# ScalarE's prelude reordered: the square root's table first, the small tanh behind the queries' copies, one table for logarithm and exponential

## The chip, the cores and the metric

The kernel is one program on one core of a Trainium2 chip. The metric is device time in microseconds, from launch to the end of the program, lower is better. The kernel before took 744.48 us as the median of three runs (744.48, 745.78 and 743.02). One execution, the one of 743.02 us, was also recorded by the hardware profiler.

The core has five engines that each work through their own queue of instructions in order: TensorE (PE, matrix products and transposes into PSUM), VectorE (DVE), ScalarE (ACT), GpSimd (POOL) and SyncE (SP, which here issues all transfers). They meet only at semaphores: one instruction counts a semaphore up when it ends (`then_inc`), another engine's queue stands still until the count is reached (`wait_ge`).

## The reference, cut to what matters

Inputs: `x` and `ctx` are 32 sequences of 128 tokens with 128 features in float32. Four blocks are added to `x` one after the other, each scaled by the tanh of one scalar gate (`g_xattn[0]`, `g_ffn[0]`, `g_xattn[1]`, `g_ffn[1]`):

1. an mLSTM attention of LayerNorm(x) over ctx, with eight heads of width 16, gates capped by 15 tanh(p/15), a cumulative sum of log-sigmoids, and a norm over each head;
2. a quantized two-layer network with a gelu (hidden width 512);
3. a dynamic-time-warping alignment of ctx to LayerNorm(x): distances, a recursion over rows, a walk back;
4. a network of eight gated experts (hidden width 512, gelu).

What this case is about is the beginning of block 1:

```python
pre = gate_in @ ifgate_w.T + ifgate_b          # gate_in: [LayerNorm(x), ctx, ctx]
pre = GATE_SOFT_CAP * jnp.tanh(pre / GATE_SOFT_CAP)
log_fg = jax.nn.log_sigmoid(f_pre)             # here as -ln(1 + exp(-f))
x = x + jnp.tanh(g_xattn[0]) * _L0_xattn_ref(_layernorm(x), ctx_1024, ctx_1024, ...)
```

## The kernel before

The kernel runs its stages one after the other over all 32 sequences. Each engine's queue is written out by hand, in one function per engine (`@block.sync`, `@block.gpsimd`, `@block.scalar`, `@block.vector`, `@block.tensor`); there is no planner. Groups `g` are of four sequences, so there are eight. A tile of a group is 128 partitions by 512 columns.

The prelude (the first 62 us) makes the inputs of the attention loop. SP issues the loads: `x` and `ctx` in four chunks each (L289, L290), nine small tensors after the first chunks (L293). VectorE takes the statistics of the first 16 sequences (L841, then `ln_stats`, L741 to L747, which ends with `bn_done`), copies the turned small tensors (L846 to L848), touches `tgr` (L849, `tg_in_ready`), waits for the square root in `ln_scales` (L751), takes the reciprocal (L759) and applies the norm to 16 sequences (`ln_apply`, recorded as L735, `ln_done` after every four). The same follows for the second half of the sequences.

TensorE turns four groups of ctx (`turn_ctx`, L1364), forms the first sums of the gates from them (`ctx_sums(0)`, L1380), turns two more groups of ctx, four groups of the normed x (`turn_x`, L1372), the last two of ctx, and forms the other sums (`query_sums`, L1388). `turn_ctx(g)` waits from g = 2 on for `k_kept`, the copy two groups back, as both use the same PSUM bank.

ScalarE's queue in the prelude is what the change touches. In order: the tanh of the four scalar gates (L447, behind a wait for `tg_in_ready`), then `keep_ctx` of groups 0 and 1 (L450, copies of the turned ctx from PSUM), the square root of the first half (L443, behind `bn_done`), `keep_ctx` 2 to 5, `keep_queries` 0 to 3 (L455, two masked copies each), `keep_ctx` 6 and 7, the second square root, `keep_sums(0)` (L460), `keep_queries` 4 to 7, `keep_sums(1)`, and then the gates: tanh (L479), exponential (L481) and logarithm (L482) of the gate values, 16 squares (L485), four roundings (L495), one masked copy (L497), a named table load (L498), an exponential (L500), and two scalings (L503, L504).

ScalarE evaluates functions from a table of which one set is active at a time. A function that is not in the active set needs an instruction ACT_TABLE_LOAD before it. `act.preload_act_table_set(name)` puts one there by name; where the program names none and one is needed, it is put in when the program is compiled. Copies, squares and scalings follow every load of this trace without a load of their own.

Behind the gates: VectorE and TensorE make a cumulative sum (L1417), the running maxima (L893), and two matrices for the attention loop. TensorE runs 16 matmuls on constants in `keep_warm` (L1342) and then waits for `mblk_ready`, `part_ready` and others before the first `exponents(0)` (L1445). `mblk` is made by VectorE in four instructions at L917, recorded as L735 with output Bm.

Of the kernel before, what the change touches and what calls it, by code (L numbers as in the profile page):

```python
# [12 lines left out]
ACT = mybir.ActivationFunctionType  # L13
# [42 lines left out]
def program(nc, x, ctx_, g_x, g_f, if_w, if_b, on_w, a_w1, a_b1, a_w2, a_b2, gate_w, m_w1, m_b1, m_w2, m_b2, out):  # L56
    with ExitStack() as stack:
        def sb(name, shape, dt=F32):
            return stack.enter_context(nc.sbuf_tensor(name, shape, dt))
# [98 lines left out]
        tgr = sb("tgr", [P, 4])  # L158
        tg = sb("tg", [P, 4])
# [74 lines left out]
        def bank(n, a=0, b=512):  # L234
            return PS[:, n, a:b]
# [191 lines left out]
        def _(act):  # L427
            steps = [0]

            def link(ins):  # L430
                steps[0] += 1
                ins.then_inc(S["act_step"], 1)
                act.wait_ge(S["act_step"], steps[0])
# [9 lines left out]
                    act.activation(lnt[:, 5, 16 * h:16 * h + 16], lnt[:, 4, 16 * h:16 * h + 16], ACT.Sqrt, bias=cst[:, 0:1]).then_inc(S["ln_sqrt"], 1)  # L443

            act.sem_inc(S["h_gelu"], 4)
            act.wait_ge(S["tg_in_ready"], 1)
            act.activation(tg[:], tgr[:], ACT.Tanh).then_inc(S["tg_ready"], 1)  # L447
            def keep_ctx(g):
                act.wait_ge(S["c_turned"], g + 1)
                act.activation(kT[:, 512 * g:512 * g + 512], bank(2 + g % 2), ACT.Copy).then_inc(S["k_kept"], 1)  # L450

            def keep_queries(g):
                act.wait_ge(S["q_turned"], g + 1)
                for r in range(2):
                    ins = act.activation(qTm[:, r, 512 * g:512 * g + 512], bank(g % 2), ACT.Copy, scale=pm[:, r:r + 1])  # L455
                ins.then_inc(S["q_kept"], 1)

            def keep_sums(n):
                act.wait_ge(S["gates_summed"], n + 1)
                act.activation(sums[:, n], bank(4 + n), ACT.Copy).then_inc(S["gates_kept"], 1)  # L460
# [12 lines left out]
            keep_sums(0)  # L473
            for g in range(4, G4):
                keep_queries(g)
            keep_sums(1)

            act.wait_ge(S["gates_biased"], 1)
            act.activation(pre, pre, ACT.Tanh, scale=1.0 / GATE_CAP).then_inc(S["gates_capped"], 1)  # L479
            act.wait_ge(S["gates_capped"], 1)  # L480
            link(act.activation(nlf, pre[:, :, NH:2 * NH], ACT.Exp, scale=-GATE_CAP))  # L481
            act.activation(nlf, nlf, ACT.Ln, bias=cst[:, 3:4]).then_inc(S["nlf_ready"], 1)  # L482
            act.wait_ge(S["gates_turned"], 2)
            for b in range(B // 2):
# [10 lines left out]
                    act.activation(fl(av_cut, w), fl(av_res if r else av, w), ACT.Copy).then_inc(S["cut_done"], 1)  # L495
            act.wait_ge(S["left_over"], 3)
            act.activation(fl(av_part, 0), fl(av_res, 0), ACT.Identity, scale=pm[:, 4:5]).then_inc(S["part_ready"], 1)  # L497
            act.preload_act_table_set("natural_log_exp_and_others")  # L498
            act.wait_ge(S["m_tok_ready"], 1)
            act.activation(expnm[:], expnm[:], ACT.Exp).then_inc(S["expnm_ready"], 1)  # L500

# [1240 lines left out]
```

## Time and profile before

| what | value |
|---|---|
| median of three runs | 744.48 us |
| the profiled execution | 743.02 us |
| its span, first to last instruction | 741.1 us |
| PE busy | 569.4 us (77%) |
| DVE busy | 569.1 us (77%) |
| ACT busy | 408.5 us (55%) |
| POOL busy | 128.3 us (17%) |
| shares of the chain that ended last | PE 63%, DVE 25%, ACT 6%, issue 3% |
| mean granted clock of TensorE, 0 to 1 | 0.88 |

The span is the time between the first and the last instruction; the 1.9 us around it are launch and end. Busy shares are means over stages with different limits. In the rows further down a line of the timeline reads: start in us from the span's start, duration of the group, engine, line, operation, output, input, count, and in brackets the engine's idle time before it with what ended it. A count above one means that neighbouring instructions of a line are merged.

### The profile page before, as it was taken

To read this page: it belongs to the slowest core of one execution; us is meant where nothing else is said; L and a number is where in the kernel's file an instruction comes from. 1 tells how busy PE (TensorE), PEld (TensorE's weight loads), DVE (VectorE), ACT (ScalarE), POOL (GpSimd) and SP (SyncE) were. 2 spreads that over 40 slices of the span, in tenths; PEclk is the share of its full clock that TensorE was granted. 3 is DMA by queue.
4 is the path that set the end of the run, shared out by engine and by line. 5 is a ranking of instruction groups with operands and counts; after the bars stand their busy time and mean duration, and the time that the engine had idled before them with its cause. 6 is when DMAs were issued, how large, how long until landed. Compare 5 with 4: busy or idle time off the path is not lost.

```text
span 741.1 us, 17115 instructions
## 1 busy us (share of the span) xinstructions
PE 569.4 (77%) x6351; PEld 402.0 (54%) x6419; DVE 569.1 (77%) x1737; ACT 408.5 (55%) x766; POOL 128.3 (17%) x163
## 2 busy tenths in 40 slices
PE   2758998826544720083679999999999999999997
PEld 2433444312244620073576777777777777777776
DVE  6867788998969559997974566586877888887775
ACT  2667876678862532265445565665545454545452
POOL 3000343413000000000036777700000000000000
PEclk9959999957858975578758999999999999999999
DMA  8100000000010000041000000000000000010000
GB/s 227 42 0 1 3 3 2 2 0 0 1 56 2 2 2 0 0 119 54 0 1 1 2 1 2 2 1 2 16 1 3 14 0 15 0 42 0 15 1 16
DMA packets 19676, 12.13 MB, mean 16 GB/s; under 512 B 1149, under 2 KB 18457, under 8 KB 19609
## 3 DMA queue, kind: packets, MB, share of 16 engines
q1 hardware_dynamic: 19608, 11.25, 5.5%
q8 instruction: 40, 0.66, 0.4%
q14 instruction: 28, 0.22, 0.1%
HBM read 9.15 MB, written 2.10 MB: 15 GB/s over the span
## 4 chain that ended last, share of the span: by engine, by line
PE 63%; DVE 25%; ACT 6%; issue 3%; SPq 1%; DMA 1%; another core or an unknown queue 0%; DVEq 0%
PE PS L1649 9%; PE PS L1664 8%; PE PS L1666 8%; PE PS L1665 8%; PE PS L1650 7%; PE PS L1648 6%; DVE A L1175 3%; DVE Bm L1146 3%; PE PS L1459 3%; PE PS L1469 2%; DVE Bm L735 2%; PE PS L1577 1%; PE PS L1478 1%; DVE A L1140 1%; ACT A L455 1%
## 5 line engine op out<-in xcount | busy, mean ns | idle before, releaser
L698 ACT ACTIVATE A<-PS,small_t 128x512 f32<-128x512 f32 x256 | 168.1, 688 | 119.0 <-PE PS L1650 117.5
L1666 PE MATMUL PS<-kT_w,A 128*128 128x128 bf16 x1024 | 174.8, 219 | 0.0
L1665 PE MATMUL PS<-kT_w,A 128*128 128x128 bf16 x1024 | 174.8, 219 | 0.0
L1664 PE MATMUL PS<-kT_w,A 128*128 128x128 bf16 x1024 | 174.7, 219 | 0.0
L1277 DVE TENSOR_TENSOR A<-A 128x512 bf16<-128x512 f32 x192 | 123.6, 690 | 7.8 <-ACT A L698 6.6
L1664 PEld LDWEIGHTS PS<-kT_w,A 128*128 128x128 bf16 x1024 | 100.2, 98 | 7.4
L1665 PEld LDWEIGHTS PS<-kT_w,A 128*128 128x128 bf16 x1024 | 100.2, 98 | 7.4
L1666 PEld LDWEIGHTS PS<-kT_w,A 128*128 128x128 bf16 x1024 | 100.2, 98 | 0.0
L1649 PE MATMUL PS<-A,xn_w 128*128 128x512 bf16 (+1 forms) x256 | 97.5, 381 | 3.5 <-issue 0.2
L1650 PE MATMUL PS<-A,xn_w 128*128 128x512 bf16 (+1 forms) x256 | 97.5, 381 | 0.0
L1285 DVE SCALAR_TENSOR_TENSOR xs<-PS,A,xs 128x128 f32 (+1 forms) x192 | 54.1, 343 | 49.2 <-PE PS L1666 49.1
L1648 PE MATMUL PS<-A,xn_w 128*128 128x512 bf16 (+1 forms) x193 | 73.5, 381 | 0.0
L413 POOL TENSOR_TENSOR A<-A 128x512 bf16<-128x512 f32 x64 | 64.5, 1040 | 22.4 <-ACT A L698 22.4
L1650 PEld LDWEIGHTS PS<-A,xn_w 128*128 128x128 bf16 x256 | 25.1, 98 | 30.7 <-issue 0.8
L1585 PE MATMUL PS<-identf,Bm 64*64 64x64 f32 x2 | 0.6, 298 | 51.6 <-DVE Bm L1146 51.6
L1648 PEld LDWEIGHTS PS<-A,xn_w 128*128 128x128 bf16 x256 | 26.7, 104 | 21.1 <-issue 0.6
L1649 PEld LDWEIGHTS PS<-A,xn_w 128*128 128x128 bf16 x256 | 25.1, 98 | 21.1 <-issue 0.6
L409 POOL TENSOR_TENSOR A<-A 128x512 bf16<-128x512 f32 x8 | 9.4, 1183 | 153.3 <-ACT A L691 153.3
L1585 PEld LDWEIGHTS PS<-identf,Bm 64*64 64x64 f32 x2 | 0.2, 125 | 51.9 <-issue 49.1
L1459 PE MATMUL PS<-A,kT_w 32*128 32x256 f32 x256 | 25.4, 435 | 3.7 <-DVE A L928 3.7
L702 ACT ACTIVATE Bm<-PS 128x512 f32 x16 | 9.6, 597 | 33.3 <-PE PS L1666 33.3
L928 DVE TENSOR_TENSOR A<-Bm,PS 128x512 f32<-128x512 f32 x32 | 20.6, 684 | 7.7 <-ACT Bm L510 4.8
(337 smaller groups left out, 1141.5 us busy)
## 6 DMA issues: line engine op xcount, KB each, us to landing
slab<-in_L_ffn_w_dram SPq DMA_DIRECT2D x16, 256.0 KB, 3.0
xs<-in_x_dram SPq DMA_DIRECT2D x4, 512.0 KB, 5.7
cs<-in_ctx_dram SPq DMA_DIRECT2D x4, 512.0 KB, 6.5
out_dram<-xs SPq DMA_DIRECT2D x8, 256.0 KB, 2.5
Bm<-in_L_ffn_W_dram SPq DMA_DIRECT2D x2, 256.0 KB, 2.9
b2blk<-in_L_ffn_b_dram SPq DMA_DIRECT2D x12, 4.0 KB
onw_b<-n_L_xattn_outnorm_w_dram SPq DMA_DIRECT2D x1, 64.0 KB
ab_b<-in_L_ffn_b_dram SPq DMA_DIRECT2D x1, 64.0 KB
```

Source lines behind the costliest of these rows:

```text
L413: pool.tensor_tensor(hl[:, e % 2, c, :], hf[:, e % 2, c, :], hh[:, e % 2, c, :], ALU.subtract).then_inc(S["h_low_pool"], 1)
L698: act.activation(hf[:, e % 2, c, :], bank(c), ACT.Gelu_apprx_tanh, bias=b1).then_inc(S["h_gelu"], 1)
L1146: dve.tensor_tensor_scan(rt[:, s + 1, 1:RTW], mins[:, s], dd[:, s], rt[:, s + 1, 0:1], ALU.min, ALU.add).then_inc(S["row_done"], 1)
L1277: dve.tensor_tensor(hl[:, e % 2, c, :], hf[:, e % 2, c, :], hh[:, e % 2, c, :], ALU.subtract).then_inc(S["h_low_dve"], 1)
L1285: ins = dve.scalar_tensor_tensor(out=row, in0=bank(4 + e % 2, P * k, P * k + P), scalar=gate, in1=row, op0=ALU.mult, op1=ALU.add)
L1459: ins = pe.matmul(PS[:, 2 + r, 0:256], kT[rows, P * b:P * b + P], qTm[rows, :, P * b:P * b + P], start=True, stop=True)
L1648: pe.matmul(bank(c), w1h[:, e, c, :], x4h[:, xw], start=True, stop=False)
L1649: pe.matmul(bank(c), w1h[:, e, c, :], x4l[:, xw], start=False, stop=False)
L1650: pe.matmul(bank(c), w1l[:, e, c, :], x4h[:, xw], start=False, stop=True).then_inc(S["h_ready"], 1)
L1664: pe.matmul(o, hh[:, e % 2, c, t], w2h[:, e, c, :], start=(c == 0 and k == 0), stop=False, skip_group_check=True)
L1665: pe.matmul(o, hh[:, e % 2, c, t], w2l[:, e, c, :], start=False, stop=False, skip_group_check=True)
L1666: ins = pe.matmul(o, hl[:, e % 2, c, t], w2h[:, e, c, :], start=False, stop=(c == NC - 1), skip_group_check=True)
```

## The change

ScalarE's queue is changed in three places; no other engine's is. The first instruction is now a load of the set `sqrt_and_others` in place of the wait for `tg_in_ready` with the small tanh. The small tanh stands between `keep_queries(7)` and `keep_sums(1)`, behind a load of `exp_and_others`. The load of `natural_log_exp_and_others` stands between the gates' exponential and their logarithm, and the one ahead of L500 is gone.

```diff
             act.sem_inc(S["h_gelu"], 4)
-            act.wait_ge(S["tg_in_ready"], 1)
-            act.activation(tg[:], tgr[:], ACT.Tanh).then_inc(S["tg_ready"], 1)
+            act.preload_act_table_set("sqrt_and_others")
+
             def keep_ctx(g):
...
             keep_sums(0)
             for g in range(4, G4):
                 keep_queries(g)
+            act.preload_act_table_set("exp_and_others")
+            act.wait_ge(S["tg_in_ready"], 1)
+            act.activation(tg[:], tgr[:], ACT.Tanh).then_inc(S["tg_ready"], 1)
             keep_sums(1)
...
             link(act.activation(nlf, pre[:, :, NH:2 * NH], ACT.Exp, scale=-GATE_CAP))
+            act.preload_act_table_set("natural_log_exp_and_others")
             act.activation(nlf, nlf, ACT.Ln, bias=cst[:, 3:4]).then_inc(S["nlf_ready"], 1)
...
             act.activation(fl(av_part, 0), fl(av_res, 0), ACT.Identity, scale=pm[:, 4:5]).then_inc(S["part_ready"], 1)
-            act.preload_act_table_set("natural_log_exp_and_others")
             act.wait_ge(S["m_tok_ready"], 1)
             act.activation(expnm[:], expnm[:], ACT.Exp).then_inc(S["expnm_ready"], 1)
```

The result of the small tanh (`tg`, `tg_ready`) is first read by VectorE at L962 and L963, behind `mblk`.

## Rows read from the trace of the kernel before

**Rows 1.** The chain of waits: start us, duration us, engine, output, line

```profile
13.07 0.96 DVE lnt L743
15.38 1.06 ACT kT_w L450 x2
16.46 1.28 ACT L443
17.76 0.31 ACT lnt L443
...
19.18 1.94 PE PS L1380 x8
21.12 1.90 PE PS L1364 x8
...
23.91 4.74 ACT A L455 x8
28.69 1.92 PE PS L1388 x16
...
36.88 3.01 PE PS L1388 x16
...
43.27 1.28 ACT L482
...
54.94 5.07 PE PS L1342 x16
```

**Rows 2.** Timeline of ScalarE, prelude: start, duration, instruction, idle before

```profile
15.27 0.20 ACT L447 ACTIVATE tg<-tgr 128x4 f32<-128x4 f32 x1 [13.09 <-DVE tgr L849]
...
29.43 0.38 ACT L443 ACTIVATE lnt<-lnt,cst 128x16 f32<-128x16 f32 x1
...
39.92 0.60 ACT L460 ACTIVATE Bm<-PS 128x512 f32<-128x512 f32 x1 [3.09 <-PE PS L1388]
40.53 1.28 ACT L479 ACT_TABLE_LOAD   x1
42.18 0.63 ACT L479 ACTIVATE slab<-slab 128x512 f32<-128x512 f32 x1 [0.36 <-DVE slab L870]
...
59.18 1.28 ACT L498 ACT_TABLE_LOAD   x1
...
62.65 1.09 ACT L510 ACTIVATE Bm<-PS 128x512 f32<-128x512 f32 x2 [0.34 <-PE PS L1450]
```

**Rows 3.** Timeline of VectorE, prelude

```profile
14.55 0.17 DVE L747 SCALAR_TENSOR_TENSOR lnt<-lnt 128x16 f32<-128x16 f32 x1
15.09 0.15 DVE L849 COPY tgr<-tgr 128x1 f32<-128x1 f32 x1
18.10 0.25 DVE L759 RECIPROCAL lnt<-lnt 128x16 f32<-128x16 f32 x1 [2.86 <-ACT lnt L443]
27.43 0.18 DVE L747 SCALAR_TENSOR_TENSOR lnt<-lnt 128x16 f32<-128x16 f32 x1
60.00 1.67 DVE L735 TENSOR_SCALAR Bm<-A,hneg 128x1024 bf16<-128x1024 bf16 x4
```

**Rows 4.** Timeline of TensorE, prelude

```profile
10.42 1.97 PE L1364 MATMUL PS<-identf,cs 128*128 128x128 f32 x8
16.10 1.94 PE L1364 MATMUL PS<-identf,cs 128*128 128x128 f32 x8 [3.71 <-ACT kT_w L450]
30.43 1.04 PE L1380 MATMUL PS<-kT_w,Bm 128*32 128x512 f32 x8
```

**Rows 5.** Timeline of GpSimd: copies of ctx, chunks 1 and 2

```profile
12.94 1.04 POOL L350 COPY Bm<-cs 128x1024 f32<-128x1024 f32 x1 [4.93 <-DMA cs<-in_ctx_dram]
16.58 1.04 POOL L350 COPY Bm<-cs 128x1024 f32<-128x1024 f32 x1 [2.60 <-DMA cs<-in_ctx_dram]
```

**Rows 6.** Windows: stretch, length, busy time by engine, PEclk, DMA share, GB/s

```profile
37.00:38.00 1.00, 1.00 (x12) 0.25 (x14) 1.00 (x7) 0.00 (x0) 0.00 (x0) 0.80 0.00 0
61.78:140.00 78.22, 74.04 (x1140) 35.04 (x1140) 63.40 (x140) 57.46 (x143) 27.40 (x42) 0.98 0.01 2
```

## The prediction

> **What bounds the kernel now.** I read the chain of waits first. In the prelude it stands on ScalarE from 15.38: copies of ctx, then a table load, then the first square root, and from there over TensorE and ScalarE's query copies to the gates [rows 1]. Three rows matter in it: 16.46 (the load, 1.28 us), 17.76 (the square root) and 19.18 (TensorE's sums, released by two copies behind that root). Then I read ScalarE's own timeline for what it did before 15.38. It did nothing: the small tanh at 15.27 has 13.09 us of idle time before it, ended by L849 of VectorE [rows 2]. VectorE's timeline shows what the root waited for: `bn_done` comes with L747 at 14.55 + 0.17 = 14.72, while the root starts at 17.76, and VectorE then stands 2.86 us before its reciprocal [rows 3]. So ScalarE is the late one by 3.04 us, with work that needs neither the statistics nor each other: 0.20 of tanh, the two copies (1.06) and the load (1.28), which could only start once L849 had ended at 15.24. TensorE's timeline shows the same wait from the other side: it turned two groups of ctx at 10.42, finished at 12.39, and stood 3.71 us until the first copy of ScalarE freed the bank [rows 4]. The chunk of ctx that it needs next had landed by 12.94, when GpSimd starts to copy it [rows 5].
>
> **The first edit: the root's table first, no wait.** The load of `sqrt_and_others` takes the place of the load that stands at the start anyway, under the idle 13.09 us. The copies of groups 0 and 1 then follow TensorE: the first group is turned half way through the row at 10.42, at 11.4, the second at 12.39. A pair of copies takes 1.06, so one some 0.55, and the second ends at about 13.0. ScalarE is then free 1.7 us before `bn_done`. The root starts at 14.72 plus a few hundredths for the semaphore, 14.75, in place of 17.76: **3.01 us earlier**.
>
> Does everything behind it move by as much? I follow both successors.
> - TensorE's side. Groups 2 and 3 of ctx need chunk 1 (12.94) and the copies (11.95 and 13.0), so they are turned from 12.95 to 14.9 at the duration of [rows 4] (1.94). ScalarE copies them right behind the root, which comes first in its queue; from the root's start to the sums of L1380, which those two copies release, are 19.18 - 17.76 = 1.42 us now [rows 1], so the sums start at 14.75 + 1.42 = 16.17 in place of 19.18. `small_kept` comes with L848 before L849, by 15.2, so it isn't late. The next two groups (L1364) would start at 18.1; their chunk 2 is there at 16.58 [rows 5]. Turning x follows at 20.0, and the query copies at 20.9 in place of 23.91.
> - VectorE's side. Its queue has L846 to L849 between `bn_done` and the root, which end at 15.24, and the root ends at 15.06. So the reciprocal starts at 15.27 in place of 18.10, 2.83 earlier. TensorE needs the first normed group only at 20.0, so the 0.18 by which this side moves less has no effect. One bound: VectorE's L743, a tensor_tensor of 16 columns, took 0.96 on the chain, beside GpSimd's copy at 12.94 [rows 1, 5], where L747, another small one, took 0.17 [rows 3]. The copies at 16.58 and some 3.8 us later now fall on the normed groups and possibly on the statistics behind them, so up to 2 x 0.8 = 1.6 us could be added to VectorE. The second half's L747 ended at 27.61 and its root started at 29.43 [rows 2, 3]: a slack of 1.82 now, 1.82 - 0.18 = 1.64 after the shift. The bound just fits, and I take none of it, since one such stall must already be in the rows of before.
>
> From 20.9 on every row of the chain has its predecessor 3.0 earlier and no transfer is near: the last chunks of x and ctx are needed where TensorE and VectorE are already behind them. The term is 3.01. Its bounds: if ctx chunk 1 were late for groups 2 and 3 the copies would wait for TensorE, and at worst nothing but VectorE's wait would go; then TensorE would end at its old time, a gain of nothing (0). At the upper end TensorE's clock comes up earlier, which is the first rival.
>
> **The second edit: tanh behind the queries' copies.** Added are a load (1.28, the duration of any such row) and the tanh (0.20), 1.5 us together, where ScalarE stands 3.09 us before `keep_sums(1)`, waiting for TensorE's L1388 [rows 2]. That cover is 3.01 us of matmuls, of which the clock takes a part: the first such set took 1.92 [rows 1], and even then 1.5 fits. Without any cover it would cost 1.5. It also takes away the load at 40.53. That one ended at 41.81, and the tanh behind it waited until 42.18 for VectorE, so it was hidden with 0.37 to spare: gain 0, or up to 0 again if TensorE gets faster. The wait for `tg_in_ready` is met since 15.24. Behind it nothing new is queued that waits. The readers of `tg` come after `mblk`, 20 us later. Cost of the edit: 0.
>
> **The third edit: one table for ln and exp.** At L482 a load of 1.28 stands between exponential and logarithm on the chain [rows 1], and a named load of 1.28 stands there after the change: 0, or a few hundredths for the order of wait and load. At L498 a load goes: ScalarE reaches L510 by 1.28 us earlier. But L510 was waiting for TensorE already (0.34), TensorE's first matrices wait for `mblk` of VectorE, which ends at 60.00 + 1.67 = 61.67, and VectorE's chain there doesn't wait for ScalarE's L500 before that [rows 2, 3]. So 1.28 us off the path, gain 0; upper bound 1.28, lower 0. So of the five loads in the first 62 us three are left, and just one of the two that go was worth something, through its place.
>
> The Trainium skill (ScalarE: Activation LUTs, "What ACT_TABLE_LOAD costs") puts a switch of sets at about 2.66 us, of which 1.28 are the load and 1.38 a drain. The trace has the first part only: the load at 16.46 starts 0.02 after the copies' end and the root follows 0.02 after the load [rows 1]. By the page the sum would be an estimated 4.4 us in place of 3.0; the measured gaps decide against it.
>
> **The sum.** 3.01 + 0 + 0 = 3.0 us. The profiled execution would go from 743.02 (span 741.1 and 1.92 around it) to 740.0, span 738.1. That execution was the fastest of the three and lies 1.46 under the median, so the median goes from 744.48 to **741.5 us**, 0.40% faster. What a measurement of this kernel can tell from no change is about 0.5%, 3.7 us; the three runs of before span 2.8 us. So the forecast is faster, and on the near side of that bound.
>
> **Rivals.**
> 1. *The clock comes up earlier, more than 3.0.* TensorE's durations show two levels: L1380 takes 1.94 at 19.18 and 1.04 at 30.43, the same four matmuls in two passes, near the ratio of 1.2 to 2.4 GHz [rows 1, 4]. The granted clock is recorded as 1.00 in both, so before 37 the durations have to be read. Before the change 3.71 us of idle time lie ahead of the row at 16.10; after it TensorE works from 10.42 to 12.39, 12.95 to 14.9 and from 16.17 on, with gaps of 0.6 and 1.3. If it comes to the upper level by 16.2, L1380 and L1364 save 0.9 each. ScalarE's own order takes part of that back, so I price it at 1.2: 740.3. The Trainium skill (TensorE: Matmul & The Clock Gate, "The HAM clock gate") ties the clock to how busy the engine has been lately, which speaks for this; the trace has the rise only behind the longest unbroken stretch, as that from 19.18.
> 2. *Slower: the attention loop starts at the lower level.* The 16 constant matmuls (5.07 us) end at 60.01 and bring the clock up, and the loop runs at 0.98 with 74.04 of 78.22 us busy [rows 1, 6]. The clock had fallen in 37 to 38 (0.80), behind a thin stretch. If with the shift the loop started low, each us of it at half speed would lose half a us; against the gain of 3.0 it decides from 6.0 us of low clock on, and at 9 us it costs 4.5: 746.0. For it: the level does change with what went before. Against it: the constant matmuls and the wait behind them move together with all before them, so the pattern stays the same.
> 3. *The 3 us are given back.* The copies move, but something that I hold to be early is late: chunk 2 of ctx, or VectorE's stall beyond 1.64. Then 1 to 3 us of the gain are lost: 743.5. Against it: the arrivals in [rows 5].
> 4. *It doesn't do what it says:* the compiler adds loads of its own around the named ones, as before a copy that it assigns elsewhere. Two more loads on the chain give 741.5 + 2.6 = 744.1. Against it: copies follow each of the loads of before without one.
>
> **How the numbers follow.** Forecast 0.60, rival 1 0.20, rival 2 0.04, rival 3 0.11, rival 4 0.05. The median of a few runs adds about 1 us either way. The likeliest's own range is 740.4 to 742.6. The range to hold 8 in 10 leaves out the slowest tail and the fastest: 739.5 to 743.9. Faster by over 0.5% means under 740.76: most of rival 1 (0.17 of 0.20) and a quarter of the forecast (0.15), 0.32. Slower by over 0.5% means over 748.2: rival 2's tail, 0.03. Within: 0.65.
>
> **What would show it.** Right: a load at 0.9 and no tanh until about 33.8; the root at 14.75; L1380 at 16.2; the query copies at 20.9 and 29.1; load and tanh inside the idle time before `keep_sums(1)`; TensorE's first L1445 at 58.8, set by `mblk`; L510 behind it with more idle time than now. Wrong: a second row of L1364 later than 13.0; VectorE's first L735 on x much longer than before; the second root less than 2.9 earlier; more than three loads before L510; L1445 earlier by other than 3.0; or a loop whose first blocks run at half speed.

## The result, and the profile after

The changed kernel takes 739.02 us as the median of 22 runs (736.08 to 743.06). The kernel before, run beside it and counted with its first three, takes 743.37 us as the median of 22 (740.45 to 745.78). The ratio is 0.9947, with a 95% interval from 0.9935 to 0.9959: 3.9 us faster, 3.0 to 4.8. The plain difference of the two means is 4.1 us, that of the medians 4.35; the ratio is worked out another way and differs from them by a few tenths. The forecast was 741.5 us, with a range from 739.5: too high by 2.5 us. Of these 1.1 are the base (three runs of before had a median of 744.48, all 22 have 743.37), and 1.35 that the medians differ by 4.35 in place of 3.0. The ratio's interval begins at 3.0, so the times alone don't show that there is more than 3.0. Two executions of the last series, one of the kernel before (853.91 us) and one of that kernel with its idle stretch filled (3109.82 us), were in a slow state and are left out of every ratio and mean.

The profiled execution of after took 738.34 us, its span is 736.5. Its chain of waits in the prelude (start, duration, engine, output, line; ScalarE's lines keep their numbers up to L475 and stand three or four further down behind it, those of the other engines three):

```profile
14.56 0.18 DVE lnt L750
14.77 0.31 ACT lnt L443
15.07 0.98 ACT kT_w L450 x2
16.05 0.14 issue
16.19 1.94 PE PS L1383 x8
18.12 1.91 PE PS L1367 x8
20.06 0.60 ACT kT_w L450
20.66 4.71 ACT A L455 x8
25.41 1.92 PE PS L1391 x16
...
33.60 3.51 PE PS L1391 x16
...
40.04 1.28 ACT L485
...
51.70 4.80 PE PS L1345 x16
```

Against [rows 1]: no table load is left ahead of the first root, which starts at 14.77 in place of 17.76, 2.99 earlier (3.01 forecast). The first sums start at 16.19 in place of 19.18, 2.99 (3.01 forecast). The query copies start at 20.66 in place of 23.91, 3.25 and not 3.01: between them the first eight transposes of x took 1.21 in place of 1.60, as TensorE's clock rose a little earlier in the work. L1391 at 33.60 is 3.28 earlier.

ScalarE's own timeline of after answers to [rows 2]. The first row here is of the kernel before: it too begins with a load, which ends long before the first copy. The rows behind it are of after.

```profile
0.89 1.28 ACT L447 ACT_TABLE_LOAD   x1 [0.89 <-PEq L1729]
```

```profile
0.89 1.28 ACT L446 ACT_TABLE_LOAD   x1 [0.89 <-PEq L1732]
11.77 0.60 ACT L450 ACTIVATE kT_w<-PS 128x512 f32<-128x512 f32 x1 [9.59 <-PE PS L1367]
12.56 0.60 ACT L450 ACTIVATE kT_w<-PS 128x512 f32<-128x512 f32 x1 [0.19 <-PE PS L1367]
14.77 0.31 ACT L443 ACTIVATE lnt<-lnt,cst 128x16 f32<-128x16 f32 x1 [1.61 <-DVE lnt L750]
...
26.15 0.38 ACT L443 ACTIVATE lnt<-lnt,cst 128x16 f32<-128x16 f32 x1
...
33.57 1.28 ACT L476 ACT_TABLE_LOAD   x1
34.86 0.20 ACT L478 ACTIVATE tg<-tgr 128x4 f32<-128x4 f32 x1
37.13 0.60 ACT L460 ACTIVATE Bm<-PS 128x512 f32<-128x512 f32 x1 [2.07 <-PE PS L1391]
38.94 0.63 ACT L482 ACTIVATE slab<-slab 128x512 f32<-128x512 f32 x1 [1.21 <-DVE slab L873]
...
59.41 1.08 ACT L513 ACTIVATE Bm<-PS 128x512 f32<-128x512 f32 x2 [1.77 <-PE PS L1453]
```

The reader sees the idle time change its releaser: the 13.09 us that VectorE's L849 ended are now 9.59 that TensorE's first transposes end, and the root waits 1.61 for the statistics, which are the late ones now. The moved load and tanh (33.57 to 35.06) leave 2.07 us idle before `keep_sums(1)`. ScalarE waits 1.77 at L513 in place of 0.34: the load that went from there bought idle time. VectorE's side, at the start and over the statistics of the second half:

```profile
15.16 0.24 DVE L762 RECIPROCAL lnt<-lnt 128x16 f32<-128x16 f32 x1
15.44 4.91 DVE L738 TENSOR_SCALAR xn_w<-xs,lnt 128x128 f32<-128x128 f32 x16
...
23.69 0.18 DVE L746 TENSOR_TENSOR lnt<-bns 128x16 f32<-128x16 f32 x1
24.39 0.17 DVE L750 SCALAR_TENSOR_TENSOR lnt<-lnt 128x16 f32<-128x16 f32 x1
```

The loop starts at 58.53 in place of 61.78, 3.25 earlier. The spans differ by 741.1 - 736.5 = 4.6 us, so 1.35 of this pair's difference lies behind the loop's start. The experiments are about this: is there more than 3.0, and where from.

### The profile page after: what moved, and what is told of

Its sections match the earlier page's. It is cut to its first block, busy times and chain, and to the rows that moved or that the text cites. A ratio compares the mean times of both kernels' runs of the same rounds, so it can differ in the third digit from the quotient of the medians.

```text
span 736.5 us, 17181 instructions
## 1 busy us (share of the span) xinstructions
PE 574.9 (78%) x6419; PEld 402.7 (55%) x6419; DVE 568.8 (77%) x1737; ACT 406.3 (55%) x764; POOL 128.4 (17%) x163
## 4 chain that ended last, share of the span: by engine, by line
PE 64%; DVE 25%; ACT 7%; issue 2%; SPq 1%; DMA 1%; DVEq 0%
PE PS L1669 8%; PE PS L1668 8%; PE PS L1667 8%; PE PS L1651 8%; PE PS L1652 8%; PE PS L1653 7%; DVE A L1178 3%; DVE Bm L1149 3%; PE PS L1462 3%; PE PS L1472 2%; ACT A L595 2%; DVE Bm L738 2%; PE PS L1481 1%; PE PS L1580 1%; DVE A L1143 1%
## 5 line engine op out<-in xcount | busy, mean ns | idle before, releaser
L1652 PE MATMUL PS<-A,xn_w 128*128 128x512 bf16 (+1 forms) x256 | 97.8, 382 | 0.0
L1653 PE MATMUL PS<-A,xn_w 128*128 128x512 bf16 (+1 forms) x256 | 97.7, 382 | 0.0
L1651 PE MATMUL PS<-A,xn_w 128*128 128x512 bf16 (+1 forms) x256 | 97.7, 382 | 0.0
```

Source lines behind the costliest of these rows:

```text
L1651: pe.matmul(bank(c), w1h[:, e, c, :], x4h[:, xw], start=True, stop=False)
L1652: pe.matmul(bank(c), w1h[:, e, c, :], x4l[:, xw], start=False, stop=False)
L1653: pe.matmul(bank(c), w1l[:, e, c, :], x4h[:, xw], start=False, stop=True).then_inc(S["h_ready"], 1)
```

## The experiments

Each kernel was timed beside the kernel before on one chip. "Against before" is the difference of mean times in us, with the ratio and its 95% interval behind it. The changed kernel itself stands at -4.1 (22 runs) and -4.5 (6 runs); all 28 have a mean of 739.14 and a standard deviation of 2.0, so their mean is known to 0.8 or so. "Slower than the changed kernel" compares with these 28.

**The wait put back.** The copies wait for `tg_in_ready` again, with the table loaded first:

```diff
             act.preload_act_table_set("sqrt_and_others")
+            act.wait_ge(S["tg_in_ready"], 1)
```

> The changed kernel with the wait for tg_in_ready put back ahead of the ctx copies; the root's table is still loaded first and the small tanh still stands behind the queries' copies. Theory A (the prelude's chain shifts by what the first root shifts, 3.0 us, of which 1.28 + 0.20 are load and tanh and the rest the wait): copies 0 and 1 start at 15.26 in place of 11.8 and 12.6, the root at about 16.35 in place of 14.77, so 1.6 us of the gain are lost: about 1.6 above the changed kernel, 1.6 to 2.5 below the one before, the first L1448 at 60.1. Rival B (only the load mattered, the wait is hidden by the statistics): the root stays at 14.8 and the time equals the changed kernel's.

Measured: 741.81 us median, against before -0.9 (0.9992, 0.9976 to 1.0008). The root came at 16.09, so the load and the tanh gave 1.67 of the root's 2.99. But little of it arrived. TensorE's timeline of this kernel:

```profile
10.28 1.97 PE L1368 MATMUL PS<-identf,cs 128*128 128x128 f32 x8
15.86 1.94 PE L1368 MATMUL PS<-identf,cs 128*128 128x128 f32 x8 [3.62 <-ACT kT_w L451]
18.58 1.94 PE L1384 MATMUL PS<-kT_w,Bm 128*32 128x512 f32 x8 [0.78 <-ACT kT_w L451]
```

TensorE still stands 3.62 us until the first copy frees a bank, its transposes then take 1.94, and the sums start at 18.58, 0.60 before those of [rows 1]. Both theories fall here: B, as the root moved, and A in its price, as the next thing late is the transposing, not the root. With the wait in place, load and tanh bring 0.6 of the chain's 3.0 us; the other 2.4 need the wait to go. The opposite case, no wait but the load still ahead of the root on the chain, wasn't run.

**The third edit alone**, on the kernel before:

```diff
+            act.preload_act_table_set("natural_log_exp_and_others")
             act.activation(nlf, nlf, ACT.Ln, bias=cst[:, 3:4]).then_inc(S["nlf_ready"], 1)
...
-            act.preload_act_table_set("natural_log_exp_and_others")
             act.wait_ge(S["m_tok_ready"], 1)
```

> The kernel before with the third edit alone: natural_log_exp_and_others between the gates' exponential and logarithm, none ahead of L500. Theory A: ScalarE reaches L510 1.28 us earlier and waits there for TensorE; no change, 0 +- 0.4 us, ratio 1.000. Rival C (the extra beyond 3.25 us that was measured comes from this edit): 0.9 us faster, ratio 0.9988.

Measured: +0.3 (1.0007, 0.9990 to 1.0024). Theory A; rival C's 0.9988 lies outside, though only just. The timeline is clearer: ScalarE waits for TensorE at L510 for 1.77 us, where it waited 0.34 in [rows 2].

```profile
61.07 1.09 ACT L510 ACTIVATE Bm<-PS 128x512 f32<-128x512 f32 x2 [1.77 <-PE PS L1450]
```

**Without the third edit**, the same two lines undone in the changed kernel:

> The changed kernel without its third edit: the logarithm takes the table that it had before, and natural_log_exp_and_others is loaded ahead of the exponential of L500 again. Theory A: equal to the changed kernel, as ScalarE had 1.77 us idle ahead of L510 after the change and the load takes 1.28; 3 to 4.5 us below before. Rival C (the third edit carries part of the gain): 0.9 us slower than the changed kernel.

Measured: -2.9 (0.9970, 0.9953 to 0.9986). The interval overlaps the changed kernel's and includes 3.3 us; by itself it doesn't exclude a part for the third edit, the run before does. In its timeline the load is back, and what it takes is idle time (0.35 in place of 1.77):

```profile
52.76 1.28 ACT L501 ACT_TABLE_LOAD   x1
...
56.22 1.08 ACT L513 ACTIVATE Bm<-PS 128x512 f32<-128x512 f32 x2 [0.35 <-PE PS L1453]
```

Its profiled execution had a loop start at 55.35, far earlier than 58.53, and opened the question below.

**The root's table loaded late**, behind the two copies:

```diff
-            act.preload_act_table_set("sqrt_and_others")
...
             for g in range(2):
                 keep_ctx(g)
+            act.preload_act_table_set("sqrt_and_others")
             ln(0, (0,))
```

> The changed kernel with the load of sqrt_and_others moved from the start to directly behind the two ctx copies. They end at 13.1, the load would end at 14.4, and the statistics come at 14.73: theory A says that the load is hidden there as well, the root starts at 14.8 and the time equals the changed kernel's (3 to 4.5 us below before). Rival D (the place of the load is what counts, any load near the root delays it): the root at 16.1 or later, 1.3 us slower than the changed kernel.

Measured: -2.6 (0.9963, 0.9949 to 0.9978). ScalarE's timeline of this kernel says what I had missed:

```profile
11.47 1.28 ACT L449 ACT_TABLE_LOAD   x1 [11.47 <-PE PS L1367]
12.76 1.09 ACT L449 ACTIVATE kT_w<-PS 128x512 f32<-128x512 f32 x2
13.87 1.28 ACT L464 ACT_TABLE_LOAD   x1
15.16 0.31 ACT L443 ACTIVATE lnt<-lnt,cst 128x16 f32<-128x16 f32 x1
```

With no table named at the start, one is loaded ahead of the first copy, behind its wait. The copies come 1.0 later, and the root at 15.16, 0.4 later than in the changed kernel. So a load near the root is nearly hidden (rival D's 16.1 is out), but not quite in this form. The time can't tell: its interval overlaps the changed kernel's and also holds rival D's 1.3 us.

**Two more loads under the cover** of the moved tanh:

```diff
             act.preload_act_table_set("exp_and_others")
+            act.preload_act_table_set("sqrt_and_others")
+            act.preload_act_table_set("exp_and_others")
             act.wait_ge(S["tg_in_ready"], 1)
```

> The changed kernel with two more table loads (2.57 us) ahead of the moved tanh. Load and tanh now end at 35.06, and TensorE's sums end at 37.11 when its clock is low in them and at about 35.5 when it is high. With two more, ScalarE is free at 37.6. Theory A (the moved pair stands under a cover of 2.0 us, in the profiled execution): 0.5 us of the chain lost at the low clock, up to 2.1 at the high one, so 0.5 to 2.1 us slower than the changed kernel. Rival F (there is no cover, every load counts): 2.6 us slower than the changed kernel.

Measured: -1.7 (0.9975, 0.9963 to 0.9987), so some 2.3 us slower than the changed kernel. In its profile TensorE's sums (L1393, 33.46 + 3.51) end at 36.97 at the lower clock, and ScalarE comes to `keep_sums(1)` at 37.41: 0.4 lost. The mean loss of 2.3 is beyond theory A's upper end of 2.1, which it names for sums at the upper level; within the noise neither that nor rival F's 2.6 is excluded by the time. The profiles show that one load and the tanh are covered: the changed kernel has 2.07 us idle behind them when the sums run at the lower level, and still 0.53 when they run at the upper one (ahead of 35.77 in the profile of the changed kernel again, further down).

**The loop held back** by 3.1 us of VectorE's work:

```diff
-            link(ts(fl(av_part, 1), fl(av_res, 1), pm[:, 4:5], None, ALU.mult))
+            for _ in range(5):
+                link(ts(fl(av_part, 1), fl(av_res, 1), pm[:, 4:5], None, ALU.mult))
```

> The changed kernel with the start of the attention loop held back: VectorE makes the masked copy ahead of mblk five times in place of once, four more instructions of 0.75 us, 3.1 to 3.2 us in all, so L1448 starts at 61.7 as in the kernel before. Theory A (what lies behind the loop's start doesn't care when it starts; the measured extra over 3.25 us is the spread of the runs): it loses 3.1 to 3.2 us, 0.7 to 1.0 us below the kernel before as measured, and if the extra was chance, equal to it. Rival E (the later stages gain by themselves from the prelude's shift or content): it gives back only what the shift gave; if the time comes to the kernel before's within 0.4 us, the extra belongs to the shift; if 0.9 us stay, it belongs to what else differs.

Measured: 745.02 us median, +2.3 (1.0034, 1.0019 to 1.0050), that is 5.9 slower than the changed kernel where 3.2 was held. Neither theory has this, and whether the extra belongs to the shift it can't say. The windows of the first blocks show it; first the changed kernel, then this one (stretch, length, PE busy, PEclk, DMA):

```profile
62.00:70.00 8.00, 7.79 (x134) 1.00 0.01 2
```

```profile
62.00:70.00 8.00, 8.00 (x64) 0.50 0.01 3
```

```profile
60.85 0.64 PE L1449 MATMUL PS<-Bm,slab 64*64 64x512 bf16 x4 [5.31 <-DVE Bm L738]
```

TensorE stood 5.31 us ahead of the loop, the clock fell to the lower level, and the loop did half the matmuls in the same 8 us. It took 82.7 us from the first start to the last at L1449, where the changed kernel's took 79.4: 3.3 lost. This is the mechanism of my slower rival, real, with its price, though the change didn't cause it: in the profile of after the loop starts at the upper level.

**Kept busy ahead of the loop**, 24 in place of 16 constant matmuls, on both kernels:

```diff
-            keep_warm(7, 16)
+            keep_warm(7, 24)
             pe.wait_ge(S["m_tok_ready"], 1)
```

> The changed kernel with 24 in place of 16 matmuls on constants ahead of the loop, so that TensorE works until just before L1448. Theory J (the loop takes 79.4 us, or 81.5 when the clock falls in its first blocks; the fall comes from the idle time of about 2 us ahead of it): the loop always takes 79.4, the mean lies about 1 us below the changed kernel's and the runs spread less. If the added matmuls run at the lower level they end at 62 and cost up to 2 us. Rival K (the fall has nothing to do with that idle time): no change.

> The kernel before with the same 24 matmuls. Theory J: 0.5 to 1 us below before, less spread. With the lottery of the loop's start out of both, the changed kernel's lead over this one is the prelude's alone: theory A says 3.0 to 3.3 us; with the earlier rise of the clock in a part of the runs 3.5 to 4.

Measured: the changed kernel with it -4.2 (0.9941, 0.9923 to 0.9958), the same as without; the kernel before with it -1.0 (0.9987, 0.9974 to 1.0000). In both profiles the loop took 79.3. The two differ by 742.28 - 739.04 = 3.2 us, known to 1.2 or so. That is what theory A says for the prelude alone and below the 3.5 to 4 forecast for a share of early rises; within its noise it decides nothing. In the other profiles the loop takes 79.3 to 79.5 in seven that have 1.68 to 2.04 us idle ahead of it, and 81.4 to 81.6 in six that have 2.21 to 2.44 and in one that has 1.69; two stand apart, the loop held back (82.7) and the trimmed version further down (80.3, with no idle time ahead). So the loop's time is a lottery too. Its slow case goes with the longer idle time, but that is not shown as the cause: in those six the 16 constant matmuls ahead took 4.61 to 4.84 us and in the seven 5.00 to 5.37, so the idle time is longer because the clock had come up sooner in them, and either can be what counts. That the bridge gains by it is not shown by the time of either kernel.

**The changed kernel again**, for more draws:

> The changed kernel itself once more, beside the next three on one chip. Two kernels with the same chain so far gave 2.6 and 2.9 us below before (12 runs each), it gave 4.1 in the mean of its 22 runs. Theory A (the chain's 3.25 us and the rest chance): 3.3 us below before, ratio 0.9956. Rival E (0.9 us more are real): 4.1 us, ratio 0.9945. Its trace is a further draw of the clock: either the upper level from L1383 on (loop at 55.3 as in one execution) or not (58.5 to 59.0).

> The changed kernel, one more profiled execution. Theory L: the loop starts between 55.3 and 59.0 as the clock falls out, in the mean of all such looks about 3.6 us before the kernel before's (60.2 to 62.4); L1383 takes 1.94 or, in the early case, 1.06.

> The changed kernel, a further profiled execution; as for the look before it.

Measured: 737.61 us median of 6 (0.9939, 0.9916 to 0.9963); the two single profiled executions took 740.22 and 735.68. TensorE's timeline of the second one:

```profile
10.56 1.97 PE L1367 MATMUL PS<-identf,cs 128*128 128x128 f32 x8
13.04 1.59 PE L1367 MATMUL PS<-identf,cs 128*128 128x128 f32 x8 [0.51 <-DMA cs<-in_ctx_dram]
16.29 1.06 PE L1383 MATMUL PS<-kT_w,Bm 128*32 128x512 f32 x8 [1.66 <-ACT kT_w L450]
17.29 1.09 PE L1367 MATMUL PS<-identf,cs 128*128 128x128 f32 x8
18.22 1.04 PE L1375 MATMUL PS<-identf,xn_w 128*128 128x128 f32 x8
...
31.99 1.92 PE L1391 MATMUL PS<-A,Bm 128*32 128x512 f32 x16 [1.59 <-ACT A L455]
```

The second pair of ctx groups takes 1.59, the first sums 1.06 in place of 1.94, at the same start. The clock had come up already during the transposes, in 13.04 to 14.63, where TensorE stood idle in the kernel before (12.39 to 16.10, [rows 4]). The loop started at 55.39. The first single execution has it too (1.92, then 1.07), and so had the kernel without the third edit (1.78, then 1.06).

**The kernel before again, and with its idle stretch filled:**

> The kernel before, one more profiled execution. Theory L: L1380 takes 1.94, never 1.06, since 3.7 us of idle time lie ahead of the third group of ctx; the loop starts between 60.2 and 62.4. Rival M: the early rise is seen here as well.

Measured: 743.59; L1380 took 1.93, the loop started at 60.71.

```diff
             for g in range(4):
                 turn_ctx(g)
+                if g == 1:
+                    keep_warm(7, 8)
             ctx_sums(0)
```

> The kernel before with 8 matmuls on constants in TensorE's idle stretch from 12.4 to 16.1, between the second and the third group of ctx; nothing of ScalarE's order is changed. Theory L (the change does two things: it moves the chain by 3.0 us, and by closing this stretch it lets TensorE's clock rise before the first sums in a part of the executions, which is the extra): L1383's counterpart L1380 takes 1.04 to 1.5 in place of 1.94 in most executions, and the time falls by 0.5 to 2 us below before. Rival M (the stretch has nothing to do with it, the extra is chance or lies in later stages): no change, ratio 1.000.

Measured: 0.9988 (0.9968 to 1.0009). In time this settles nothing. In TensorE's timeline it does:

```profile
13.22 2.96 PE L1342 MATMUL PS<-neg,identb 128*128 128x512 bf16 x8
17.16 1.07 PE L1364 MATMUL PS<-identf,cs 128*128 128x128 f32 x8 [0.97 <-ACT kT_w L450]
20.23 1.07 PE L1380 MATMUL PS<-kT_w,Bm 128*32 128x512 f32 x8 [2.01 <-ACT kT_w L450]
```

With the stretch filled, the transposes take 1.07 in place of 1.94 and the sums 1.07 in place of 1.94, with ScalarE's order unchanged. So, in this one execution, work in the idle stretch was enough to bring the clock up for them. The sums themselves start no earlier, as they now wait longer for ScalarE (2.01 before L1380, 1.14 without the filling), but what follows them does. The traces can be laid side by side if the start is counted from TensorE's first transposes of ctx, as these vary by 1.2 us with the loads' arrival:

| profiled executions | first sums take | second query sums start, us behind the first transposes of ctx |
|---|---|---|
| order of before (before, third edit alone, bridged, before again) | 1.93 to 1.94 | 26.27 to 26.46 |
| before with the stretch filled | 1.07 | 24.51 |
| wait put back | 1.94 | 26.00 |
| changed order, clock not up early (after, held, two more loads, bridged, again) | 1.94 | 23.05 to 23.60 |
| changed order, clock up early (without third edit, both single executions) | 1.06 to 1.07 | 21.43 to 21.59 |
| TensorE kept busy (three versions, further down) | 1.06 to 1.07 | 21.54 to 21.93 |

The order of ScalarE's work is worth 3.0 us here (26.36 to 23.31 in the means; with the root's table loaded late it is 23.64), and the early rise some 1.8 more, in either order.

**TensorE kept busy in the whole prelude**, first the early part, then the gaps between the gates too, then the same trimmed. The diff is of the trimmed one, on the changed kernel; the early part is its first three places:

```diff
+            keep_warm(7, 16)
             pe.wait_ge(S["small_in"], 16 * 9)
...
                 turn_ctx(g)
+                if g == 1:
+                    keep_warm(7, 4)
+            keep_warm(7, 8)
             ctx_sums(0)
...
+            keep_warm(7, 6)
             query_sums(1)
             turn_sums(1)
             spread(0)
+            pe.wait_ge(S["scale_ready"], 1)
+            keep_warm(7, 3)
             pe.wait_ge(S["nlf_ready"], 1)
...
+            keep_warm(7, 8)
             pe.wait_ge(S["a_ready"], 1)
...
+            keep_warm(7, 10)
             for j in range(2):
                 pe.wait_ge(S["m_ready"], 4 * (j + 1))
...
-            keep_warm(7, 16)
+            keep_warm(7, 34)
```

> The changed kernel with TensorE kept busy by matmuls on constants early in the prelude: 16 from 3.7 us on, 4 between ctx groups 1 and 2, 8 ahead of the first sums. Theory G (the clock is at its lower level from 10 to 20 us because TensorE was idle before): L1383 takes 1.04 in place of 1.94, L1367 1.04 in place of 1.97, the query copies start 1.5 to 2 us earlier than 20.66, then VectorE's statistics at 24.56 limit the second root to 24.6 in place of 26.15; together 1.5 us faster than the changed kernel. Rival H (the durations are not the clock's): no change, or slower by the added matmuls.

> As the one before, and constants' matmuls in the later gaps of the prelude too: 6 ahead of the second query sums, 6 behind the spread, 10 behind the cumulative sum, 10 ahead of the turned maxima, 26 in place of 16 ahead of the loop. Theory G: L1391 1.9 in place of 3.5, L1398 0.6, L1420 0.6 in place of 1.24, L1424 1.04 in place of 1.98, L1429 0.6 in place of 1.12; 3 to 4 us more, in all 4 to 5.5 us faster than the changed kernel, and it varies less from run to run if the clock makes the spread. Rival H: no change. Rival I (the added matmuls run at the low clock and stand in the way): slower by up to 3 us.

> The version with TensorE busy through the whole prelude, trimmed: 3 in place of 6 behind the spread (those 6 ended at 40.1 and put the cumulative sum off by about 1 us), 8 in place of 10 behind it, 34 in place of 26 ahead of the loop. Theory G and J: the loop starts at about 54.9 and takes 79.4: 2.5 to 3 us below the untrimmed version, at 735 us. Rival I: the added matmuls get in the way, equal or slower.

Measured: the early part 738.4 us median (0.9937, 0.9916 to 0.9957), all gaps 737.45 (0.9922, 0.9903 to 0.9940), trimmed 736.68 (0.9916, 0.9900 to 0.9932). All three have L1383's counterpart at 1.06 or 1.07 as theory G says, and the second root at 24.7 to 25.0 in place of 26.15. The first eight transposes of ctx, 1.97 in every other kernel, take 1.09. The gain in time is smaller than forecast: against before they stand at -4.6, -5.7 and -6.3, so 0.5, 1.6 and 2.2 below the changed kernel's mean of -4.1, where 1.5, 4 to 5.5 and about 4 were forecast. Trimming brought 0.6 of the 2.5 to 3 forecast for it. The trimmed version is the fastest of the study. Its interval doesn't meet the one of the changed kernel's 22 runs (0.9935 to 0.9959), but overlaps that of its 6 runs on the same chip (0.9916 to 0.9963), so that it beats the changed kernel is likely and not settled. Its timeline ahead of the loop:

```profile
47.66 7.50 PE L1345 MATMUL PS<-neg,identb 128*128 128x512 bf16 x34
55.12 0.41 PE L1457 MATMUL PS<-Bm,slab 64*64 64x512 bf16 x4
```

The loop starts at 55.12 (54.9 forecast) without an idle gap, at the upper level. It then takes 80.3 us and not the 79.4 forecast: the granted clock is 0.66 in 115 to 125 us, inside the loop, where it is 1.00 in before and 0.88 in after. In the version with all gaps filled it is 0.83 in 55 to 65, and the loop takes 81.4. Why is open.

## Why the prediction was wrong, point by point

- *The first edit, 3.01 us:* right in size and place. The root moved by 2.99, the sums by 2.99, and over all profiles the second query sums by 3.0. Its two sides came as worked out: chunk 1 of ctx released TensorE, and VectorE's reciprocal followed its own copies (15.16, forecast 15.27). The bound of 1.6 us for VectorE beside GpSimd didn't come: its 16 normed tiles took 4.91 in place of 5.00, and L746 of the second half 0.18.
- *How the 3.01 divide:* I named 0.20 of tanh, 1.28 of load and the copies held by the wait, and in the expectation for the wait put back I took each as worth its length. With the wait put back, the first two bring 0.6 at the sums, since TensorE's transposes stand behind the same copies.
- *The second edit, 0:* right. 1.5 us under a cover that left 2.07, or 0.53 with the sums at the upper level; two loads more no longer fit.
- *The third edit, 0:* right. It moved idle time at L510 from 0.34 to 1.77.
- *The base, 744.48:* this step failed. The median of three runs was taken as it stood, though the profile was of an execution 1.46 lower. The 22 runs have 743.37, 1.1 lower, of the 2.5 us by which the forecast missed. With 743.37 the same sum gives 740.4, and a range moved with it begins at 738.4, below the measured 739.02.
- *The sum, 3.01 + 0 + 0:* this step failed too. It is short by a term, TensorE's clock, which it took as unchanged; the earlier rise stood as rival 1, priced at 1.2 us with a chance of 0.20. The row on which it rested was the 3.71 us of idle time before 16.10 [rows 4]. In the nine profiled executions with the changed order of the prelude and nothing added early on TensorE, three have the first sums at 1.06 or 1.07 and six at 1.93 or 1.94. So the rise does come early in a part of the executions. In the five where that gap is still there (3.51 to 3.71 us; the four with the order of before and the one with the wait put back) none has it. Five draws without it would come by chance in one case of eight if the share were a third there too, so that it comes with the change rests as well on the filled stretch (one execution, 1.07) and on the place of the rise, in transposes that stand where the gap was. When it comes it is worth 1.8 us, where I had 1.2. A third of 1.8 is 0.6, an estimate from few draws, which makes 3.0 + 0.6 = 3.6. The interval of the times, 3.0 to 4.8, holds this and also 3.0 alone; the bridged pair gave 3.2. With 3.6 and the old base the forecast would be 740.9, and a range moved with it would begin at 738.9, 0.1 below the measured time.
- *What is left:* the medians differ by 4.35, 0.75 more than 3.6. The plain means differ by 4.1, and nothing on record ties the rest to a cause; it is within the noise.
- *The other rivals:* a lower clock in the loop's first blocks is real (81.5 in place of 79.4 us), but seen with both orders; nothing was given back; and no load was added around the named ones, though one is where none is named.

What came behind the loop's start in this pair, 1.35 us, is not the change's. The time from the loop's last L1448 (L1445 in before) to the end of the span is 598.5 to 600.0 us in all profiled executions but one (601.6, the early part kept busy), with either order: 600.0 in this pair's before, 598.6 in its after. Within it the matmuls that turn the distances (L1577 in before, L1580 in after) take 12.3 to 14.2 us in kernels that don't differ there, 13.9 in the pair's before and 12.5 in its after, which is the whole of it. What makes that stretch vary is open; no run was made on it.

## What to carry to other kernels

When a wait goes, look at every engine that stood behind it, not only at the one on the chain: a TensorE that no longer stands idle early on may run its next matmuls at the upper level, which was worth 1.8 us here in the executions that had it, on top of the 3.0 of the chain. A load or a small function costs by its place: the same 1.28 us was worth nothing where it ended in a wait, and little where the next engine still stood behind the same copies, so undo one part at a time before saying which brought the gain. And a base of three runs that spread over 0.4% is no base for a forecast of 0.4%.

## What the runs showed of the hardware that was not expected

- The same program draws its clock. The first sums of the changed kernel take 1.06 or 1.07 with 1.33 to 1.66 us idle ahead, and 1.94 with 1.28 to 1.34. The second query sums take 1.92 or 3.0 to 3.6, with 1.59 or 1.60 us idle ahead in either case (only the two fullest versions have 0.30). The loop takes 79.4 or 81.5. The runs of the changed kernel spread over 7 us (736.08 to 743.06).
- The recorded clock reads 1.00 from the start of the program until its first fall, though the durations in 10 to 20 us are those of the lower level: eight transposes take 1.97 us there, 1.04 at 23.66, and 1.09 already at 10.19 when 16 constant matmuls run ahead of them. In that stretch only durations tell.
- A plain copy as the first activation gets a table load of 1.28 us if none is named ahead of it, and that load stands behind the copy's wait (11.47, in the version with the root's table loaded late).
